# Gathers that pass over rows outside a visit's block of nodes, in a two-layer graph attention kernel

## What is computed

```
h = relu(layernorm(x))
x = x + GAT(h):   e = leaky_relu(a_src[src] + a_dst[dst]);  alpha = softmax of e over the edges of each dst
                  out[dst] = sum(alpha * h[src])
h = relu(layernorm(x))
x = x + TR(h):    score = q[dst].k[src] / 4 + edge_attr @ We + be;  softmax over the edges of each dst
                  out = layernorm(sum(attn * v[src]) @ Wo + bo + h) * gamma + beta
```

## Time and profile before

| | |
|---|---|
| median of 3 runs | 1489.5 us (1488.92 to 1489.5) |
| the profiled execution's own time | 1486.06 us |
| its span, first to last instruction | 1484.3 us |
| POOL busy | 1190.4 us, 80% of the span |
| PE / DVE / ACT busy | 980.2 / 929.5 / 636.9 us (66% / 63% / 43%) |
| gathers L511 | 880, 870.6 us busy |
| spacers L497 | 880, 297.1 us busy |
| packets of the gathers' queue | 91.12 MB, 23.5% of 16 DMA engines' span |

### The profile page before, as it was taken

One profiled execution on the slowest core, in us unless ns is written; L12 is line 12 of the kernel. 1 busy time (PEld: TensorE's weight loads), 2 busy tenths in 40 slices (PEclk: granted clock), 3 DMA queues, 4 the chain that ended last, 5 costly groups with the idle time before them and its releaser, 6 DMA issues.

```text
span 1484.3 us, 21963 instructions
## 1 busy us (share of the span) xinstructions
PE 980.2 (66%) x4985; PEld 817.4 (55%) x4985; DVE 929.5 (63%) x3002; ACT 636.9 (43%) x1699; POOL 1190.4 (80%) x1806
## 2 busy tenths in 40 slices
PE   5547557777667776676575766676676856566674
PEld 4335446656555565564355655666565746455564
DVE  6446556665665666567834666666666666666578
ACT  5624343453434434341367343444445344444404
POOL 5888888888888888884048888888888888888820
PEclk9655555555555555555686778786867688787765
DMA  6332222222223222222133333333333233333311
GB/s 141 72 69 47 71 49 53 63 71 48 70 48 70 48 69 48 63 48 75 57 112 93 89 88 90 86 89 89 90 89 88 87 89 89 89 89 87 89 29 44
DMA packets 54209, 110.41 MB, mean 74 GB/s; under 512 B 16876, under 2 KB 30848, under 8 KB 53956
## 3 DMA queue, kind: packets, MB, share of 16 engines
q0 software_dynamic: 36288, 91.12, 23.5%
q1 hardware_dynamic: 16483, 17.39, 4.3%
q10 hardware_dynamic: 1313, 0.50, 0.1%
HBM read 100.60 MB, written 8.81 MB: 74 GB/s over the span
## 4 chain that ended last, share of the span: by engine, by line
POOL 39%; issue 6%; DVE 5%; PE 3%; ACT 1%; DMA 0%; DVEq 0%; POOLq 0%; SPq 0%; ACTq 0%
POOL G L511 29%; POOL pad_i L497 10%; PE bank L851 2%; DVE halves L1074 1%; DVE acc L1432 1%; DVE PV L1405 0%; DVE mv L1081 0%; DVE G L1572 0%; DVE hn L1580 0%; DVE xs L1526 0%; DVE hn L1525 0%; DVE hn L1524 0%; PE bank L899 0%; DVE G L1569 0%; DVE hn L1523 0%
## 5 line engine op out<-in xcount | busy, mean ns | idle before, releaser
L511 POOL DMA_INDIRECT G<-table,idx_all x880 | 870.6, 989 | 143.2 <-issue 124.0
L851 PE MATMUL bank<-PV,S 128*125 128x144 f32 x1760 | 446.0, 413 | 135.8 <-DVE PV L1405 74.8
L851 PEld LDWEIGHTS bank<-PV,S 128*125 128x125 f32 x1760 | 369.5, 284 | 164.1 <-issue 121.4
L1432 DVE TENSOR_TENSOR acc<-acc,bank 125x144 f32 x880 | 259.5, 295 | 235.1 <-PE bank L851 154.8
L497 POOL MEMSET pad_i<- 1x300 int32 x880 | 297.1, 338 | 18.8 <-DMA table<-h0b 9.8
L615 ACT ACTIVATE S<-iota_n,lid 128x125 f32<-128x125 f32 x880 | 275.8, 387 | 0.5 <-DVE pen L1169 0.5
L834 PE MATMUL bank<-qe,ST 125*128 x880 | 144.5, 316 | 40.1 <-DVE prod L1225 22.7
L1405 DVE TENSOR_TENSOR PV<-G,PV 128x512 f32<-128x512 f32 x220 | 150.2, 684 | 19.6 <-issue 19.4
L619 ACT ACTIVATE S<-S,ones 128x500 f32<-128x500 f32 x220 | 156.6, 712 | 7.2
L628 ACT ACTIVATE ST<-bank 125x512 f32<-125x512 f32 x110 | 62.6, 596 | 218.7 <-PE bank L899 119.1
L834 PEld LDWEIGHTS bank<-qe,ST 125*128 125x128 f32 x880 | 126.2, 221 | 50.5 <-issue 49.5
(11 more groups left out here) (220 smaller groups left out, 1257.9 us busy)
## 6 DMA issues: line engine op xcount, KB each, us to landing
G<-table,idx_all POOLq DMA_INDIRECT x880
prod<-in_edge_attr_dram SPq DMA_DIRECT2D x8, 672.0 KB
table<-G SPq DMA_DIRECT2D x12, 224.0 KB
bias_rows<-qe SPq DMA_DIRECT2D x1, 1664.0 KB, 5.8
table<-h0b SPq DMA_DIRECT2D x8, 178.5 KB
out_dram<-G SPq DMA_DIRECT2D x8, 168.0 KB
prod<-in_edge_attr_dram SPq DMA_DIRECT2D x8, 90.0 KB
xs<-in_x_dram SPq DMA_DIRECT2D x1, 504.0 KB
```

The lines of the kernel that those rows point to most:

```text
L511: pool.indirect_dma_start(G[:, u, v, 0:w], None, table, bass.IndirectOffsetOnAxis(ap=idx_all[:, g * GV + v:g * GV + v + 1], axis=0)).then_ ...
L851: last = pe.matmul(sums_bank(p)[0:BN, at:at + H * SLOT], S[:, ur, v, :], PV[:, v, :, :].rearrange("p h k -> p (h k)"), start=True, stop=True)
L1432: ve.tensor_tensor(a, a, o, ALU.add).then_inc(s.sem["acc_added"], 1)
```

## The change

A new pass on DVE ahead of layer 1 rewrites `idx_all` for the visits from 48 on (groups 3 to 27). It clamps `lid` to 0 to 124, compares the result with `lid` (1 where they differ, so 1 for a foreign row), multiplies by 4096 times the partition's number and adds that to the index. A foreign row on partition p gets its index plus 4096 p; on partition 0 that adds nothing, so a foreign row there is still fetched. Every gather carries a bound: an index over 3,124 raises no error, and that row is passed over, so its place in `G` keeps what was there. POOL waits for the pass at the first quarter of group 3 in layer 1. The first three groups of both layers fetch all their rows, under the bound too.

```diff
+        s_masked = sem("foreign_rows_masked")
...
                 for g in range(GROUPS):
                     u = g % UNROLL
+                    if n == 0 and g == UNROLL:
+                        pool.wait_ge(s_masked, 1)
                     for j in range(quarters(g)):
...
                             pool.indirect_dma_start(
                                 G[:, u, v, 0:w], None, table,
-                                bass.IndirectOffsetOnAxis(ap=idx_all[:, g * GV + v:g * GV + v + 1], axis=0)
+                                bass.IndirectOffsetOnAxis(ap=idx_all[:, g * GV + v:g * GV + v + 1], axis=0),
+                                bounds_check=NODES - 1, oob_is_err=False
                             ).then_inc(s_gath[u][j], 16)
...
             ve.wait_ge(s_vte, 8)
             ve.wait_ge(s_bz, 16)
+            foreign = PV[:, :, :, :].rearrange("p v h k -> p (v h k)")[:, 0:VISITS - UNROLL * GV]
+            later = slice(UNROLL * GV, VISITS)
+            ve.tensor_scalar(CC[:, 0:1], vcol_[:, 0:1], float(P * 32), None, op0=ALU.mult).then_inc(s_v, 1)
+            n_v[0] += 1
+            then(ve.tensor_scalar(foreign, lid[:, later], 0.0, float(BN - 1), op0=ALU.max, op1=ALU.min))
+            then(ve.tensor_tensor(foreign, foreign, lid[:, later], ALU.not_equal))
+            ve.scalar_tensor_tensor(idx_all[:, later], foreign, CC[:, 0:1], idx_all[:, later], op0=ALU.mult,
+                                    op1=ALU.add).then_inc(s_masked, 1)
```

## The result

The changed kernel takes 1532.7 us (median of 4 runs, 1530.57 to 1533.67) against 1489.5 (1488.92 to 1489.56): a ratio of 1.029, 95% interval 1.0278 to 1.0302, or 43.2 us more. Forecast were 1512.4 us and a range of 1479 to 1552. The sign and the place were right; of 43.2 us more, 22.9 had been forecast, about half. The profiled execution took 1532.46 us.

What follows compares the result with a forecast made beforehand. POOL's pace through its instructions was taken to bound both loops. To the profiled 1486.06 us came 22.9 for the bound and 0 for moves, wait, DVE pass and rows; with 3.4 us up to the median, 1512.4 us, range 1479 to 1552.

Steps and rivals of the forecast that it cites:

- The sign: Whole kernel: slower, by 1.5%; slower had a chance of 0.50, faster 0.30, no measurable change 0.20.
- the place: On POOL, in all 880 gathers of both loops: the median gather would go from 952 ns to about 978.
- a saving per row: POOL's gathers from group 3 on: forecast 0; the rival took 1.66 ns (9.7 us) to 7.44 ns (43.4 us), chance 0.30.
- register moves: On POOL, 880 moves hidden behind gathers: forecast 0; the rival had them exposed at 0.07 us each, 62 us, chance 0.05.
- A gather with a bound: On POOL, the index test in all 880 gathers: 26 ns each, +22.9 us, with 71 ns as upper end.

## What to carry to other kernels

Where one engine works through hundreds of equal instructions without a pause, cost a change by what it does to that one instruction, fixed part included, and not by the bytes it saves elsewhere. An option that lets rows be left out is paid by every gather; here it would have had to be cheaper than a saving per row that turned out to be zero. Look at what is put between those instructions too, register moves and spacers alike: the largest gain in this kernel, a tenth, was in taking out an instruction that computes nothing. And compare means as well as medians: a gather that overlaps another engine's instruction can last nearly twice as long.

## What was not expected

- A gather with a bound: 50 to 55 ns more at 128 rows, 39 at 64, and 69 with the bound as an error (at 128 rows), on 952 ns (912 at 64).
- A row passed over costs POOL as much as a row fetched (1002 ns with and without half of the rows), and its queue keeps its 36,288 packets.
- A gather that starts while DVE weighs a quarter is longer by what is left of the weighing, less 0.12 to 0.13 us.
- Register moves that each fit into a gap still cost 9 us through 13 gaps, most of them 72 gathers apart. Such gaps aren't the moves' alone: with no moves there are, beside the first gather's, eight with a spacer of 236 elements, 0.1 us longer than the usual 0.16, nine with 120, 0.3 us longer, and nine of up to 1.45 us with 64 rows asked for. With 300 elements, 128 rows and no moves only the first gather has one. What the sequencer waits for in them stays open.
- Part of the pace of the kernel before was its spacers': 338 ns of 1.45 us a visit did no work, and the kernel is 10% faster without them.
